# Copying the attention accumulator out of PSUM on VectorE instead of ScalarE, in a fused attention and coupling-network kernel

## What is computed

```python
# per sequence: 16 query heads of 8, 4 key/value heads, causal, two half-heads each
q, k = rotary(rms_norm(x @ Wq.T)), rotary(rms_norm(x @ Wk.T));  q = q * q_gain
v = (x @ Wv.T) * sigmoid(x @ Wg.T)
a1, a2 = causal_attn(q1, k1, v1), causal_attn(q2, k2, v2)      # halves of 4
y = concat([a1 - lambda * a2, a1 + lambda * a2]) @ Wo.T
x = layernorm(x + y)
# coupling network, three cycles
gf = global_net(mean over tokens of x)
for _ in range(3):
    out = out + (0.1 + range * (0.7 * gf + 0.3 * coupling_net(out) - 0.5) * 2) * twist(out)
x = layernorm(x + out)
```

## Time and profile before

| | |
|---|---|
| median of 3 runs | 284.07 us (283.53 to 285.05) |
| the profiled execution: time | 283.17 us |
| the profiled execution: span from its first to its last instruction | 281.4 us |
| TensorE busy | 248.3 us, 88% |
| ScalarE busy | 235.6 us, 84% |
| VectorE busy | 198.5 us, 71% |
| GpSimd busy | 77.6 us, 28% |
| the 16 accumulator copies, on ScalarE | 0.605 us each in the median |

### The profile page before, as it was taken

The page is one execution under the profiler, slowest core; times in us unless marked ns, Lnnn a source line. Parts: engine busy times, 40 slices in busy tenths (PEclk is TensorE's granted clock), DMA queues, the critical chain, the costliest instruction groups (busy, mean ns, idle before and its releaser), DMA issues.

```text
span 281.4 us, 8388 instructions
## 1 busy us (share of the span) xinstructions
PE 248.3 (88%) x2944; PEld 110.3 (39%) x2944; DVE 198.5 (71%) x767; ACT 235.6 (84%) x339; POOL 77.6 (28%) x237
## 2 busy tenths in 40 slices
PE   3149999999999999999999999989897999999980
PEld 2023434444344343444444444434353332223880
DVE  4497557696886967869678696763253577999992
ACT  2138999999999999999999999999975878778684
POOL 6411422415224152242432424310011000000472
PEclk9999999999999999999999999999999999999995
DMA  4201451555516517145252550624300165552045
GB/s 103 81 1 32 82 114 28 109 48 143 112 29 138 104 45 149 38 92 113 74 112 47 121 113 19 130 56 81 69 1 1 40 150 131 133 126 63 9 141 151
DMA packets 58071, 23.42 MB, mean 83 GB/s; under 512 B 42784, under 2 KB 56000, under 8 KB 58048
## 3 DMA queue, kind: packets, MB, share of 16 engines
q1 hardware_dynamic: 58048, 23.13, 38.1%
HBM read 4.90 MB, written 2.10 MB: 25 GB/s over the span
## 4 chain that ended last, share of the span: by engine, by line
PE 69%; issue 12%; ACT 10%; DVE 5%; DMA 1%; ACTq 0%; POOL 0%; SPq 0%; DVEq 0%
PE O L579 12%; PE O L585 10%; PE S L692 8%; PE S L492 6%; PE S L502 4%; PE M L617 3%; PE M L604 3%; ACT o_sb L867 3%; PE S L521 3%; PE S L733 2%; PE S L482 2%; PE S L512 2%; PE M L628 2%; PE S L702 2%; PE M L611 2%
## 5 line engine op out<-in xcount | busy, mean ns | idle before, releaser
L861 ACT ACTIVATE probs_past<-S 128x1024 f32<-128x1024 f32 x64 | 64.5, 1038 | 6.2 <-PE S L482 6.2
L861 ACT ACTIVATE probs_late<-S 128x1024 f32<-128x1024 f32 x64 | 66.4, 1050 | 1.5 <-PE S L492 1.5
L579 PE MATMUL O<-probs_past,values 128*32 128x512 f32 x256 | 35.0, 616 | 6.5 <-ACT o_sb L867 5.4
L861 ACT ACTIVATE probs_early<-S 128x1024 f32<-128x1024 f32 x32 | 32.8, 1028 | 3.7 <-PE S L521 3.7
L585 PE MATMUL O<-probs_late,values 128*32 128x256 f32 x512 | 34.3, 385 | 0.2 <-ACT probs_late L861 0.2
L1078 DVE TENSOR_TENSOR roped<-rotated,rstd 128x128 f32<-128x128 f32 x64 | 12.1, 248 | 25.9 <-POOL rstd L1426 25.9
L1411 POOL TENSOR_TENSOR minus_half_sum<-sum_eps,minus_half 128x40 f32<-128x40 f32 x16 | 4.3, 268 | 83.4 <-DVE estimate L1069 83.4
L1299 DVE SCALAR_TENSOR_TENSOR cY<-coup,ratio,Y 128x256 f32<-128x256 f32 x48 | 21.0, 480 | 5.8 <-ACT coup L943 5.0
L692 PE MATMUL S<-X,cn_w 128*128 128x512 f32 x48 | 25.0, 627 | 0.0
L409 PE MATMUL M<-w_proj,xT_in 128*128 128x224 f32 x64 | 18.9, 424 | 4.6 <-DMA xT_in<-in_xT 4.0
L492 PEld LDWEIGHTS S<-qk 32*64 32x64 bf16 x512 | 8.1, 101 | 34.7 <-issue 34.7
(11 more groups left out here) (169 smaller groups left out, 526.5 us busy)
## 6 DMA issues: line engine op xcount, KB each, us to landing
Y<-X SPq DMA_DIRECT2D x48, 128.0 KB, 2.4
xT_in<-in_xT SPq DMA_DIRECT2D x16, 128.0 KB, 2.5
x_res<-in_x SPq DMA_DIRECT2D x16, 128.0 KB, 2.1
out<-result SPq DMA_DIRECT2D x16, 128.0 KB, 1.9
qk<-parts SPq DMA_TRANSPOSE x15, 4.9
future_in<-in_future SPq DMA_DIRECT2D x1, 128.0 KB, 2.4
w_o<-in_w_o SPq DMA_DIRECT2D x2, 64.0 KB, 2.0
cn_w<-in_cn_w SPq DMA_DIRECT2D x2, 64.0 KB, 2.4
```

Of the source, the lines that this page charges most:

```text
L579: mm = pe.matmul(O[32 * g:32 * g + 32, :], values[p][:, 0, g, s, at:at + 32], probs_past[:, s, g, :], start=m == 0, stop=False)
L861: act.activation(dst, S[TILE_BUFFER[n]][:, :, :], ACT.Exp).then_inc(exp_done[n], 1)
```

## The change

`copy_outputs` leaves ScalarE's program and enters VectorE's. On ScalarE it stood in `attend(b)` for batch b-1 behind `exponentials(b, 1)`, and for batch 15 behind the loop. On VectorE it stands in `attend(b)` for batch b itself, behind `add_residual(b-1)` and ahead of `split(b+2)`. It waits for the same semaphores and raises the same one. Nothing else is edited.

```diff
@@ scalar: copy_outputs removed
-            def copy_outputs(b):
-                for done in pv_done:
-                    act.wait_ge(done, b + 1)
-                reach(act, n_["o_turned"], b)
-                act.activation(o_sb[:, :], O[:, :], ACT.Copy).then_inc(n_["o_ready"], 1)
...
                 exponentials(b, 0)
                 exponentials(b, 1)
-                if not first:
-                    copy_outputs(b - 1)
                 exponentials(b, 2)
...
-            copy_outputs(BATCH - 1)
             gelu1(0, 0)
@@ vector: copy_outputs added
+            def copy_outputs(b):
+
+                for done in pv_done:
+                    dve.wait_ge(done, b + 1)
+                reach(dve, n_["o_turned"], b)
+                dve.tensor_copy(o_sb[:, :], O[:, :]).then_inc(n_["o_ready"], 1)
...
                 if not first and not general:
                     add_residual(b - 1, 1 - p, half_b - (1 - p))
+                copy_outputs(b)
                 if project_more:
                     split(b + 2)
```

## The result

The changed kernel takes **291.84 us** (median of 4 runs, 291.44 to 292.02). The kernel before takes 284.56 us (median of 4 runs, 283.53 to 285.11). The ratio is 1.0258 with a 95% interval of 1.0222 to 1.0294, so the change makes it slower by about 7.3 us. That is on the low side: the kernel before sometimes runs at a mean granted clock of 0.985 and takes 284.5 to 285.1 us, otherwise 282.5 to 283.8 us at 0.989 or more, and in later sessions its median was 283.06 to 283.48 us. The profiled execution of the changed kernel took 292.02 us with a span of 289.9 us, against 283.17 and 281.4 us, so 8.9 us more in time and 8.5 us more in the span.

What follows compares the result with a forecast made beforehand. The loop L592, copy, split, x1, L628 was to bind at 12.29 us per batch. Loop 8.0, batch 14 0.8, batch 15 -0.5 and end 0.75 make +9.0 us; from base 283.6, 292.6 us, range 288.3 to 295.3.

Steps and rivals of the forecast that it cites:

- The length of the copy: VectorE's 128x512 float32 copy from PSUM takes 0.69 us, with 0.42 as low end and 0.75 as high.
- rival 1: VectorE's copy from PSUM runs at twice the rate, 0.42 us: +5.3 us, 288.9 us; chance 0.06.
- Its start: VectorE's copy, carrying six waits, starts 0.22 us after L592 ends, bounds 0.03 and 0.35.
- The slack of 0.13 us: L628 comes 0.80 us later; 0.13 is free since the fourth exponential holds the L579 behind it, leaving 0.67 per batch.
- rival 2: L628 has unseen cover, so only VectorE's own loop of 11.96 us binds: +5.1 us, 288.7 us; chance 0.08.
- The 0.28 us on TensorE are worth nothing: Removing TensorE's 0.28 us wait ahead of the first L579 gains nothing; TensorE would wait longer for the fourth exponential.
- VectorE's own loop, 11.96 us: VectorE's work per loop batch, copy and six waits included, needs 11.96 us, under the 12.29 us of the binding loop.
- Batch 14: This batch still has a split ahead of its x1, with no hold to take off: +0.8 us.
- Batch 15: No split here, so ScalarE's relief counts; the second exponential becomes the limit: -0.5 us.
- The end: After the last L592, VectorE's copy delays sum_x1, normalize and L628; +0.75 us goes through.
- Rival 3: No change: VectorE's idle gaps ahead of L1173 and L1078 swallow the copy, 283.4 us; chance 0.09.
- rival 4: Faster: TensorE's removed wait counts in full and the delays are covered, -4.4 us, 279.2 us; chance 0.05.

Runs made afterwards that it cites:

- b: Kernel before, ScalarE still copying, plus one 128x512 float32 VectorE addition on spare tiles ahead of the split: 290.53 us, 12.04 us per batch.
- c: Changed kernel with one wait on VectorE's copy, for the last chunk of the accumulation, in place of six: 290.52 us, 12.08 us per batch.
- d: Kernel before with ScalarE's copy cut to 64 of 512 columns, for timing alone (output incomplete): 283.48 us, 11.58 us per batch.
- a: Changed kernel with turn_x1 behind the second weigh on TensorE and keep_x1 behind ScalarE's sixth exponential: 287.22 us, 11.95 us per batch.
- f: Changed kernel with turn_x1 behind the second weigh, keep_x1 behind the sixth exponential, and one wait on the copy: 288.39 us, 11.95 us per batch.
- g: Changed kernel with turn_x1 behind the second weigh, keep_x1 behind the sixth exponential, ScalarE's projection copy behind the fourth; six waits: 287.07 us.
- e: Changed kernel with sum_x1 moved from behind the split into VectorE's gap behind gate_values: 287.27 us, 11.95 us per batch.
- n: Kernel before, ScalarE copying, with sum_x1 in VectorE's gap and the normalisation inside the split behind its first three casts: 282.52 us, 11.63 us per batch.
- i: Kernel before, ScalarE copying, with turn_x1 behind the second weigh, keep_x1 behind the sixth exponential, projection copy behind the fourth: 286.04 us, 11.83 us per batch.
- m: Changed kernel with normalisation inside the split, sum_x1 in VectorE's gap, one wait in the loop, last batch's copy on ScalarE: 281.82 us, 11.59 us per batch.
- j: Changed kernel with later turn_x1, later projection copy, sum_x1 in VectorE's gap, one wait in the loop, last copy on ScalarE, keep_x1 unmoved: 283.30 us.
- h: Changed kernel with turn_x1, keep_x1 and the projection copy all later, one wait on the copy, sum_x1 in VectorE's gap: 286.49 us, 11.79 us per batch.

## Why the prediction was right

The time (291.84 against 292.6) and the mechanism both held: the loop L592, copy, split, `x`, L628 is the one that binds. In the parts outside the loop some steps were wrong, with small terms. Point by point:

- *The length of the copy.* Predicted 0.69 us, measured 0.69. The rule of the Trainium skill, "VectorE: DVE Perf Modes", section "Why PSUM operands drop a tier", is that a float32 operand in PSUM holds an instruction to the 1x rate. The trace agrees: 0.69 us against 0.66 us for b's addition of that size in SBUF. Twice the rate, rival 1, did not occur.
- *Its start.* Predicted 0.22 us after L592, measured 0.26. c shows that 0.19 of it comes with the six waits.
- *The slack of 0.13 us.* 12.28 - 11.62 = 0.66 per batch, where the prediction had 0.80 - 0.13 = 0.67. Here two small errors nearly cancel, which is luck. The split starts 0.87 us after L592 ends (143.63 to 144.50), against 0.03 before, so it is 0.84 later and not 0.80. L628 follows the end of `x` by 0.12 us, where the prediction read 0.21 as a distance without slack. So there were 0.09 us of slack more than it said, part of rival 2's case but far from the whole of it. Counted from L592, `x` comes 0.85 us later (4.51 against 3.66), L628 0.77 (5.23 against 4.46) and the L579 behind it 0.65 (5.60 against 4.95), so the 0.13 us under the fourth exponential was there, as 0.12.
- *The 0.28 us on TensorE are worth nothing.* d measured 0.04, from slightly shorter exponentials. This holds against the chain of waits, which led through the copy.
- *VectorE's own loop, 11.96 us.* a came to 11.95, but f shows the exponentials' loop at the same 11.95 in that order. The figure fits, and a alone is no proof of it. In g the exponentials come sooner and VectorE's list is unchanged, and its last eight loop batches lie at 11.95 in the mean, which supports the figure.
- *The start.* The first L592 comes 0.19 us later than before, where the prediction had nothing. a and e have the same copy and come within 0.06 us of the kernel before, and in after 0.23 us stands already at VectorE's first instruction of attention (13.42 against 13.19). So it is hardly the copy's.
- *The first loop batch.* It lengthened by 0.32 us, 11.63 to 11.95, and not by 0.67, and the second by 0.60. So the loop gave about 7.5 us and not 8.0. The prediction overlooked that the path to `x` is shorter in this batch. `sum_x1` is left out in `attend(1)`, so `x` follows the split directly, as VectorE's rows of after show:

```profile
48.70 0.22 DVE L1099 TENSOR_TENSOR parts<-rest,parts 128x64 bf16<-128x64 f32 x1
48.83 0.60 DVE L1186 TENSOR_SCALAR x<-summed,moments,ln_rstd 128x128 f32<-128x128 f32 x2
```

  L628 waits 0.45 us there and the batch takes 11.95 us, which is what e shows in every batch by taking the same instruction off the path.
- *Batch 14.* 11.51 to 12.20, so +0.69 against a predicted +0.8.
- *Batch 15.* 11.44 to 11.14, so -0.30 against -0.5. The prediction had the wrong limit: it took the second exponential, as holds in batch 14, but here the first L579 still waits 0.76 us for `o_sb`, now for VectorE's copy, and comes 2.34 us after L592 against 2.64 before.
- *The end.* Counted from the last L592, L628 came 0.80 us later, against a predicted 0.75, and the second Gelu 0.86. The first Gelu came 1.16 us later, behind its table load, and the idle time ahead of the second took that in, as foreseen. But the last L628 came only 0.50 us later, since TensorE's wait there shrank. These rows are VectorE's and TensorE's, of before and then of after:

```profile
215.99 0.25 DVE L1181 BATCH_NORM_AGGREGATE moments<-stats 128x2 f32<-128x6 f32 x2 [0.47 <-DVE stats L1177]
...
217.97 0.44 PE L628 MATMUL S<-ident,x 128*128 128x128 f32 x2 [1.17 <-DVE x L1188]
```
```profile
224.51 0.25 DVE L1179 BATCH_NORM_AGGREGATE moments<-stats 128x2 f32<-128x6 f32 x2
...
226.51 0.44 PE L628 MATMUL S<-ident,x 128*128 128x128 f32 x2 [0.80 <-DVE x L1186]
```

  That is no slack that took in the delay. In the kernel before VectorE stands idle for 0.47 us between the statistics and L1181, which starts 0.96 us after them; in after it starts 0.58 us after them. The copy's place is not the cause, since b and n have 0.59 us with ScalarE copying. The long form is in before, d and i alone, which have the same VectorE program. What makes it long is open. It gave the changed kernel 0.37 us that have nothing to do with the copy.
- *The sum.* 0.2 at the start, 7.5 + 0.7 - 0.3 in the batches and 0.5 at the end make +8.6 against a measured +8.5 us in the spans; the prediction had +9.0. The 0.2 at the start and the 0.37 us taken off at the end are not the copy's, so its own cost is about 8.8 us. The forecast of 292.6 also hangs on its base of 283.6 us, between two times of the kernel before; against the 284.56 us measured beside the changed kernel the same sum would give 293.6.

Rivals 3 and 4 fell by the wait for `x`: 9.7 us in batches 3 to 14. Rival 3's gaps on VectorE exist, but they stand behind `x`. m shows the rival's true form: the copy is nearly free once `x` is normalised ahead of part of the work that the copy delays.

**What stays open.** What makes VectorE's L1181 late at the end of before, d and i. Why m's and n's first L592 differ by 0.58 us, which hides most of what the copy brings in m; 0.36 of it stands already at VectorE's first instruction of attention (13.52 against 13.16). What c's one wait and e's sum give together, without any move on TensorE and ScalarE. Whether j's copy of `x` is the only thing between 11.75 and 11.6, which was read from its chain and not tried.

## What to carry to other kernels

Before moving work to the engine with the lower share, list what stands behind the new place on that engine and find the item that another engine takes next: here `x`, with 0.13 us of slack behind a product. A wait on the chain that ended last is worth only the distance to the next loop: 0.28 us were on the chain, and 0.04 came back when they were cut. And when a moved piece delays something urgent, reorder first on the engine that received it. m does so and reaches 11.59 us. h and j, which reorder TensorE and ScalarE instead, stay at 11.79 and 11.75, with new waits in both.

## What the runs showed of the hardware

**Some builds lose 1.7 us or more at the start.** In b, c, f and h the first L592 comes at 34.7 to 35.1 us. In before, after, a, e, g, i, j, m and n it comes at 32.6 to 33.2. (d's 34.5 comes from its late table load.) VectorE in the opening of f, and of the changed kernel, where the same four instructions run on:

```profile
13.54 0.46 DVE L1069 TENSOR_TENSOR roped<-rotated,rstd 128x128 f32<-128x128 f32 x2
15.67 0.39 DVE L1069 TENSOR_TENSOR roped<-rotated,rstd 128x128 f32<-128x128 f32 x2 [1.67 <-issue]
```
```profile
13.56 0.88 DVE L1069 TENSOR_TENSOR roped<-rotated,rstd 128x128 f32<-128x128 f32 x4
```

VectorE stops for 1.67 us and waits for nothing that the profile shows; in h it is 1.70, in c 1.81 and in b 2.13 us. The place is some 2 us behind the branch between the two forms of attention. c differs from the changed kernel only by five waits fewer, so a small edit elsewhere in VectorE's program is enough to bring the stop. Its cause is open. It takes back most of c's gain for anyone who reads totals alone. j has one wait in the loop too, but keeps six in the other form of attention, and does not show the stop.

**Six waits on one instruction cost 0.19 us more than one.** VectorE's copy starts 0.26 us after its last producer with six waits (after) and 0.07 us with one (c, and m too). The 0.19 us came back in each batch of c.

**The same two instructions can stand 0.38 us further apart.** At the end of attention L1181 of the last batch (by the numbers of the kernel before) starts 0.96 us after L1177 in before, d and i and 0.58 to 0.59 us after it in the eleven other kernels. The cause is open.

**Exponentials are slightly slower behind ScalarE's copy.** The third and fourth take 1.05 and 1.07 us in the kernel before, 1.02 and 1.03 in after and in d, whose copy is short. The projection's copy takes 0.58 us in n, where ScalarE copies the accumulator, and 0.54 in after. I have no cause for it.
